# A decoder layer on one core: the second attention's output rows as three products of hi and lo halves

## The reference, cut to what matters

```python
q = (x1 @ wq.T).reshape(b, n, HEADS, HEAD_DIM).transpose(0, 2, 1, 3)
k = (x2 @ wk.T).reshape(b, m, HEADS, HEAD_DIM).transpose(0, 2, 1, 3)
v = (x2 @ wv.T).reshape(b, m, HEADS, HEAD_DIM).transpose(0, 2, 1, 3)
dots = jnp.einsum('bhnd,bhmd->bhnm', q, k) * SCALE
attn = jax.nn.softmax(dots, axis=-1)
out = jnp.einsum('bhnm,bhmd->bhnd', attn, v)
out = out.transpose(0, 2, 1, 3).reshape(b, n, DIM)
return out @ wo.T + bo
...
x = _layernorm(x + _L0_xattn_ref(x, ctx_1024, ...))
logits = xf @ router_w + router_b     # the router reads the same x
```

## Time and profile before

| | |
|---|---|
| median of 3 runs | 1996.84 us (1996.15 to 2000.22) |
| profiled execution | 1995.04 us, of which the span is 1993.4 us |
| granted TensorE clock, mean over the span | 0.978 |
| busy: PE, DVE, ACT, POOL | 1895.2, 1222.5, 884.5, 816.2 us |
| DMA | 243.53 MB |

### The profile page before, as it was taken

The page is one execution under the profiler, slowest core; times in us unless marked ns, Lnnn a source line. Parts: engine busy times, 40 slices in busy tenths (PEclk is TensorE's granted clock), DMA queues, the critical chain, the costliest instruction groups (busy, mean ns, idle before and its releaser), DMA issues.

```text
span 1993.4 us, 26331 instructions
## 1 busy us (share of the span) xinstructions
PE 1895.2 (95%) x9904; PEld 1260.5 (63%) x9904; DVE 1222.5 (61%) x2279; ACT 884.5 (44%) x1587; POOL 816.2 (41%) x735
## 2 busy tenths in 40 slices
PE   6999999989999999999999999999969999999992
PEld 4876666677655555555445545544439999888991
DVE  5566444237678788888678778778554434444433
ACT  3212322322366566666556456556714433333431
POOL 3002200100188788888667657565021222332112
PEclk8999999999999999999999999999969999999996
DMA  7102433574477477656434424422243445454316
GB/s 249 43 1 90 149 126 123 189 215 141 142 149 177 103 168 160 146 127 156 106 90 122 107 60 128 106 65 64 75 154 103 130 132 138 101 139 110 98 20 189
DMA packets 123647, 243.53 MB, mean 122 GB/s; under 512 B 11105, under 2 KB 29297, under 8 KB 119473
## 3 DMA queue, kind: packets, MB, share of 16 engines
q1 hardware_dynamic: 108560, 185.46, 31.5%
q0 software_dynamic: 13872, 54.30, 13.7%
q10 hardware_dynamic: 1088, 2.10, 0.3%
HBM read 147.15 MB, written 62.42 MB: 105 GB/s over the span
## 4 chain that ended last, share of the span: by engine, by line
PE 82%; DVE 12%; DMA 2%; issue 1%; ACT 1%; SPq 1%; POOL 1%; ACTq 0%; POOLq 0%; DVEq 0%
PE banks L1111 35%; PE banks L1370 11%; PE banks L1277 11%; PE banks L1247 10%; PE banks L1266 8%; DVE max L1544 8%; PE banks L1298 4%; PE banks L1117 2%; DMA k_parts<-out_lo 1%; DMA wv_raw<-in_wv_t 1%; DVE stats_y L1752 0%; DMA k_half<-in_xwk_t 0%; PE banks L1185 0%; DVE src_lo L1414 0%; DVE den_c L1563 0%
## 5 line engine op out<-in xcount | busy, mean ns | idle before, releaser
L1544 DVE TENSOR_REDUCE max<-banks 128x1 f32<-128x512 f32 x1024 | 627.7, 682 | 141.2 <-PE banks L1247 140.3
L2015 POOL TENSOR_TENSOR probs<-probs,probs 128x512 f32<-128x512 f32 x464 | 582.8, 1290 | 247.9 <-PE banks L1277 247.9
L1895 ACT ACTIVATE probs<-banks 128x512 f32<-128x512 f32 x1024 | 520.2, 608 | 259.5 <-PE banks L1266 258.9
L1247 PE MATMUL banks<-k_stack,q_stack 98*128 98x512 f32 x1024 | 428.1, 425 | 2.3 <-DVE max L1544 2.2
L1266 PE MATMUL banks<-q_stack,k_stack 98*128 98x512 f32 x1024 | 376.9, 398 | 2.6 <-ACT probs L1895 2.6
L1247 PEld LDWEIGHTS banks<-k_stack,q_stack 98*128 98x128 f32 x1024 | 191.6, 187 | 192.0 <-DVE max L1544 105.9
L1277 PE MATMUL banks<-probs,v_grp 128*32 128x512 f32 x2048 | 250.8, 602 | 0.0
L1266 PEld LDWEIGHTS banks<-q_stack,k_stack 98*128 98x128 f32 x1024 | 191.7, 188 | 62.4 <-ACT probs L1895 17.9
L2061 POOL DMA_INDIRECT y_rows<-eo,tok x40 | 78.1, 1952 | 218.1 <-DVE eo L1745 161.7
L1732 DVE TENSOR_TENSOR hid_lo<-hid,hid_hi 128x640 fp32r<-128x640 f32 x64 | 52.9, 826 | 142.5 <-ACT hid_hi L1960 142.5
L2025 POOL TENSOR_TENSOR x_nat<-x_nat,bxo_row 128x512 f32<-128x512 f32 x16 | 21.1, 1352 | 268.8 <-PE banks L1117 268.8
(11 more groups left out here) (228 smaller groups left out, 2702.6 us busy)
## 6 DMA issues: line engine op xcount, KB each, us to landing
k_stack<-k_parts SPq DMA_DIRECT2D x144, 256.0 KB, 5.3
w_raw<-in_L_ffn_w SPq DMA_DIRECT2D x16, 2048.0 KB, 8.3
probs<-probs POOLq DMA_DIRECT2D x31, 1024.0 KB, 10.0
q_stack<-q_parts SPq DMA_DIRECT2D x48, 256.0 KB
v_grp<-v_rows SPq DMA_DIRECT2D x48, 256.0 KB, 3.3
raw<-in_ctx_t SPq DMA_DIRECT2D x8, 1024.0 KB, 6.7
k_parts<-out_hi SPq DMA_DIRECT2D x32, 256.0 KB, 2.5
k_parts<-out_lo SPq DMA_DIRECT2D x32, 256.0 KB, 2.9
```

Of the source, the lines that this page charges most:

```text
L1247: nc.tensor.matmul(out, queries_of(t)[:, j, tile_of(k)], keys_of(t)[0:STK + SHIFT, j, mc * HALF:(mc + 1) * HALF], start=True, stop=True) \
L1544: V.reduce_max(max4[:, tiles_of(t), :, :][:, k, j, mc:mc + 1], bank(bank_of["max", t, mc, k, j]), AX.X) \
L1895: S.activation(probs_of(t, s)[:, j, :], bank(bank_of["score", t, s, j]), ACT.Exp, scale=SCALE) \
L2015: G.tensor_tensor(a[:, j, :], a[:, j, :], b[:, j, :], ALU.add).then_inc(pair_added.sem, 1)
```

## The change: what it does

- **Stage one** loads `xwo` (W_o of the second attention) into the tile that held the raw keys' weights, splits it by ACT and DVE in the third chunk of batch one's context, and stores both halves, 1 MB each, in DRAM (`store_xwo`, on SP, behind the values of (0, 3, 1)). The gate waits for these stores too. `load_xwo` at (3, 5) loads the lo half in place of the whole; `load_xwo_hi` at (8, 0) loads the hi half into the place of `probs7`.
- **Heads** are split: ACT copies 128x512 of `heads_t` into `heads_hi` (place of `probs6`, room for one half of a batch), POOL subtracts and writes `heads_lo` over `heads_t` (`split_heads`, 15 times). The last group of the last half is split per 128 tokens, by ACT and DVE (`split_tile`, 4 times).
- **rows** is three float32r matmuls a group instead of one float32 matmul. **parts** is eight float32 matmuls in column groups instead of four, on the hi and the lo halves.
- **probs:** in batch two and the last eight tiles of batch one the exponentials use six tiles in turn. By fours ends four tiles earlier.
- **Denominators** are taken in the order of their due time.
- The split of the first half's groups 0 to 2 is a generator of its own, `first_heads`, started at (7, 7), ahead of `rows_of(0, 0)` in the queue. Other splits are AT_END steps in `rows_of` or follow a `divide`.

```diff
+PLAIN_TILES = (3, 0, 8, 5, 4, 1)
+BY_FOURS = B * NG * MT - 2 * FOUR
...
-            return t * MT + s < B * NG * MT - FOUR
+            return t * MT + s < BY_FOURS
...
+                    if (b, mc, u) == (0, 0, 0):
+                        do("load_weight", "xwo")
+                    if (b, mc) == (0, 2):
+                        do("split_weight", "xwo", u)
+                    if (b, mc, u) == (0, 3, 1):
+                        do("store_xwo")
...
+        def first_heads():
+            for g in range(NG - 1):
+                yield AT_END
+                split_heads(0, 0, g)
...
             do("route_weights", b, h)
+            yield AT_END
+            next_heads(b, h, 0)
             yield WITHOUT_PE
             do("route_slots", b, h)
+            yield AT_END
+            next_heads(b, h, 1)
             for k in range(TOPK):
                 yield WITHOUT_PE
                 do("hot", b, h, k)
+                yield AT_END
+                next_heads(b, h, 2 + k)
             yield WITH_PE
             do("table", b, h, ring=next_s_bank)
...
             do("divide", t, k)
+            if t == LAST:
+                do("split_tile", b, h, k)
             if k == HT - 1:
+                if (b, h) == (1, 1) and g < NG - 1 or g == NG - 1 and not h:
+                    split_heads(b, h, g)
...
         def denominators(until):
+            pending.sort(key=lambda due: due[0])
             while pending and pending[0][0] <= until:
...
+                if (turn, s) == (7, 14):
+                    start_side(first_heads())
+                if (turn, s) == (8, 0):
+                    do("load_xwo_hi")
...
+            step = t * MT + s
+            if not by_fours(t, s):
+                return probs[PLAIN_TILES[(step - BY_FOURS) % len(PLAIN_TILES)]]
...
-                    pe.wait_ge(*divided[turn_of[b * NG + g, h], k])
+                    pe.wait_ge(*(tile_below[b, h, k] if part == LATE else heads_below[b, h, g]))
                 pe.wait_ge(*xwo_in[()])
-                accumulate(out, [(heads_t[:, g, tile_of(h * HT + k)], xwo[:, g, :]) for g in gs], start=part != LATE) \
+                pe.wait_ge(*xwo_hi_in[()])
+                cols = tile_of(h * HT + k)
+                accumulate(out, [(heads, w[:, g, :]) for g in gs
+                                 for heads, w in ((heads_hi[:, g, tile_of(k)], xwo_hi), (heads_hi[:, g, tile_of(k)], xwo),
+                                                  (heads_lo[:, g, cols], xwo_hi))], start=part != LATE) \
...
+                by_column_groups(out, [(head_w[:, g, :], heads_hi[:, g, :].bitcast(F32)) for g in range(NG)], start=False,
+                                 stop=False)
+                by_column_groups(out, [(head_w[:, g, :], heads_lo[:, g, half].bitcast(F32)) for g in range(NG)],
+                                 start=False) \
+                    .then_inc(parts_summed.sem, 1)
...
+            def split_heads(b, h, g):
+                act.wait_ge(*divided[turn_of[b * NG + g, h], HT - 1])
+                if b or h:
+                    act.wait_ge(*parts_summed[(b, h - 1) if h else (b - 1, NH - 1)])
+                else:
+                    act.wait_ge(*den_summed[B * NG - 1, 3])
+                S.activation(heads_hi[:, g, :], heads_t[:, g, h * HALF:(h + 1) * HALF], ACT.Copy) \
+                    .then_inc(heads_above.sem, 1)
...
                 if k == 0 and b:
-                    pool.wait_ge(*xo_summed[b - 1, h, HT - 1, WHOLE])
+                    pool.wait_ge(*parts_summed[b - 1, h])
...
+            def split_heads(b, h, g):
+                half = slice(h * HALF, (h + 1) * HALF)
+                pool.wait_ge(*heads_above[b, h, g])
+                G.tensor_tensor(heads_lo[:, g, half], heads_t[:, g, half], heads_hi[:, g, :].bitcast(F32),
+                                ALU.subtract).then_inc(heads_below.sem, 1)
...
+            def store_xwo():
+                sp.wait_ge(*weight_lo["xwo", NC - 1])
+                for part, tile in enumerate(w_parts["xwo"]):
+                    Q.dma_start(xwo_parts[part], tile[:, :, :].bitcast(F32)).then_inc(xwo_out.sem, 16)
+
+            def load_xwo_hi():
+                sp.wait_ge(*den_summed[B * NG - 1, 7])
+                Q.dma_start(xwo_hi[:, :, :].bitcast(F32), xwo_parts[0]).then_inc(xwo_hi_in.sem, 16)
```

More of the change, by code:

```diff
@@ L183, in program @@
         v_grp = put("v_grp", [P, MT, P])
+        probs_at = [put.at + i * 4 * HG * HALF for i in range(9)]
         probs = [put(f"probs{i}", [P, HG, HALF]) for i in range(9)]
+        heads_hi = Shelf(nc, probs_at[6])("heads_hi", [P, NG, HALF], F32R)
+        xwo_hi = Shelf(nc, probs_at[7])("xwo_hi", [P, NC, D], F32R)
         shift_rows = put("shift_rows", [SHIFT * HG * HT, P], F32R)
@@ L192, in program @@
         heads_t = put("heads_t", [P, NG, T])
-        xwo = put("xwo_t", [P, NC, D])
+        heads_lo = Shelf(nc, tail_base)("heads_lo", [P, NG, T], F32R)
+        xwo = put("xwo_lo", [P, NC, D], F32R)
         y_nat = put("y_nat", [P, HT, D])
@@ L225, in program @@
         wo, wxq = put("wo", [P, NC, D]), put("wxq", [P, NC, D])
+        k_half_at = put.at
         k_half = put("k_half", [P, HT, D])
@@ L250, in program @@
         w_parts["ck"], w_parts["cv"] = w_parts["k"], w_parts["v"]
+        w_raw["xwo"] = k_half
+        w_parts["xwo"] = [Shelf(nc, v_half_at)("xwo_first_hi", [P, NC, D], F32R),
+                          Shelf(nc, k_half_at)("xwo_first_lo", [P, NC, D], F32R)]
         put = Shelf(nc, loop_base)
@@ L308, in program @@
         bias_in = signal("bias_in", 5 * 16)
-        w_in = {n: signal(f"w{n}_in", 16) for n in ("v", "q", "o", "xq", "ck", "cv")}
+        w_in = {n: signal(f"w{n}_in", 16) for n in ("v", "q", "o", "xq", "ck", "cv", "xwo")}
         chunk_in = signals("chunk_in", 2, 16)
@@ L406, in program @@
             "load_fold": lambda: (fold_in,),
+            "store_xwo": lambda: (xwo_out,),
             "load_xwo": lambda: (xwo_in,),
+            "load_xwo_hi": lambda: (xwo_hi_in,),
+            "split_heads": lambda b, h, g: (heads_above, heads_below),
+            "split_tile": lambda b, h, k: (tile_above, tile_below),
             "zero_counts": lambda: (counts_zero,),
@@ L700, in begin_parts, with next_heads @@
             do("parts_first", b, h)
+        def split_heads(b, h, g):
+            do("split_heads", b, h, g)
+        def next_heads(b, h, g):
+            if (b, h) == (0, 0):
+                split_heads(0, 1, g)
+            elif (b, h) == (0, 1) and g < NG - 1:
+                split_heads(1, 0, g)
+        def first_heads():
+            for g in range(NG - 1):
+                yield AT_END
+                split_heads(0, 0, g)
         def rows_of(b, h):
@@ L1083, in probs_of @@
         def probs_of(t, s):
-            four, place = divmod(t * MT + s, FOUR)
+            step = t * MT + s
+            if not by_fours(t, s):
+                return probs[PLAIN_TILES[(step - BY_FOURS) % len(PLAIN_TILES)]]
+            four, place = divmod(step, FOUR)
             return probs[(four - (0, 3, 4, 7)[place]) % len(probs)]
@@ L1323, in parts @@
                 for g in range(NG):
-                    pe.wait_ge(*divided[turn_of[b * NG + g, h], HT - 1])
+                    pe.wait_ge(*(tile_below[b, h, HT - 1] if turn_of[b * NG + g, h] == LAST else heads_below[b, h, g]))
                 pe.wait_ge(*folded[()])
-                by_column_groups(bank(bank_of["parts", b, h]),
-                                 [(head_w[:, g, :], heads_t[:, g, h * HALF:(h + 1) * HALF]) for g in range(NG)],
-                                 start=False).then_inc(parts_summed.sem, 1)
+                out = bank(bank_of["parts", b, h])
+                half = slice(h * HALF, (h + 1) * HALF)
[4 more added lines that the diff above has]
+                    .then_inc(parts_summed.sem, 1)
             def logits(b, h):
@@ L1804, in split_weight @@
                     act.wait_ge(*weight_free(name))
+                if name == "xwo":
+                    act.wait_ge(*weight_lo["cv", NC - 1])
                 S.activation(w_parts[name][0][:, c, :], w_raw[name][:, c, :], ACT.Copy).then_inc(weight_hi.sem, 1)
@@ L1896, in score, with split_tile @@
                     .then_inc(exp_done.sem, 1)
+            def split_heads(b, h, g):
[6 more added lines that the diff above has]
+                    .then_inc(heads_above.sem, 1)
+            def split_tile(b, h, k):
+                act.wait_ge(*divided[LAST, k])
+                S.activation(heads_hi[:, NG - 1, tile_of(k)], heads_t[:, NG - 1, tile_of(h * HT + k)], ACT.Copy) \
+                    .then_inc(tile_above.sem, 1)
             def copy_num(t):
```

36 lines of the change are left out of this document (26 added, 10 removed).

## The result

The changed kernel takes **2016.73 us** (median of 4 runs, 2016.55 to 2017.28), beside 1996.96 us for the kernel before (4 runs, 1996.15 to 2000.22). The ratio is 1.0096, with a 95% interval of 1.008 to 1.0112: slower by 0.8 to 1.1%, some 19 us. I had forecast 1985.1 us and given "slower" a chance of 0.04. The profiled execution has a span of 2014.4 us, 21.0 over that of before.

What follows compares the result with a forecast made beforehand. PE was taken to set the time, with 82% of the last-ending chain, DVE next. Terms of rows, parts, moves, splits, stores and tail summed to -11.7 us, from 1996.84 to 1985.1 us; range 1979.5 to 1992.

Steps and rivals of the forecast that it cites:

- Slack is left, so 0 for single splits: Loop clocks with one split: pair sums are 2.3 us early for PE's pass, so POOL's subtraction costs 0.
- I estimate the sums start 1.3 to 1.5 us later: POOL in split clocks: pair sums start that much later, behind a subtraction waiting for ACT's copy.
- The double split at (8, 0), +0.7: Two splits in one clock: the sums of (8, 1) end 2.5 us later and PE waits some 0.7 us.
- POOL becomes the bound where heads are split: Rival, 15 clocks with a subtraction: sums end behind the pass and PE waits, 19.4 us, total 2003.8; chance 0.05.
- DVE takes up the saving: Rival, rows clocks: DVE leaves no gap to spare, each clock gives back 0.4 us, total 1990; chance 0.10.
- Rows, -9.6: Twelve whole tiles of rows on PE: each saves 0.80 us by three float32r products, -9.6 us.
- Early rows: Four early tiles of the last half: each goes from 2.77 to 2.11 us on PE, -2.6 us in all.
- Parts, +2.6: Three times in the loop: eight float32 matmuls in column groups take twice the 0.88 us of four, +2.6 us.
- Moves and denominators, -2.7 and 0: Loop: later side work gains 2.0 near (14, 2) and 0.7 in the last clock; denominators' extra pass and ordering cancel.
- Stores, +0.5: Stage one: 2 MB of stores of xwo ahead of the gate cost 0.5 us; rival of 1992.8, chance 0.08.
- the upper bound: Stage one: +8.2 us if key and query stores on SP's queue wait behind the 2 MB.
- Late rows: The tail: splits are hidden, and four late tiles take 2.8 us for 3.6, -0.6 us.

Runs made afterwards that it cites:

- experiment 1: Changed kernel with POOL's 128x512 subtraction of each split cut to one column, same place and waits: 2005.01 us, ratio 1.0044.
- experiment 5: Changed kernel with POOL's subtraction of a split moved behind the clock's pair sums, ACT's copy staying in place: 2003.3 us, ratio 1.0041.
- experiment 6: Changed kernel with POOL's subtraction behind the pair sums and also cut to one column: 1985.23 us, ratio 0.9948.
- experiment 7: Kernel before plus a probe behind its last output, DVE instructions beside POOL's additions: six small ones took 7.3 us, six reductions 3.65 us.
- experiment 8: Changed kernel with splits placed by hand where POOL has room, a second high-half buffer, subtraction behind the pair sums: 1983.51 us, ratio 0.9943.
- experiments 3 and 4: Kernel before with only batch two's side work moved: 1992.81 us; kernel before with only the six tiles and the denominators' order: 1995.67 us.
- experiment 11: Kernel before with only stage one's load, split and 2 MB of stores added, gate waiting for them: 1994.31 us, ratio 1.0005.
- either probe: Experiment 7, and a second probe on the kernel before where DVE comes at 16 points of POOL's instructions: small pairs took 1.52 to 2.44 us.
- experiment 12: The changed kernel run once more, nothing altered, beside the kernel before: 2015.14 us, ratio 1.01.

## Why the prediction was wrong, step by step

**The step that failed** is in the splits: "Slack is left, so 0 for single splits." I measured POOL's slack against the one reader of its sums, PE's denominator pass 2.3 us later, and for single splits it holds roughly (PE's waits for POOL are 5.2 us in all, 2.1 of them behind the double split). But POOL's gap had a second user. In before POOL stands idle ahead of the sums of nearly every clock, and DVE's small steps run there at full speed (the chain of `rsqrt_a` takes 0.16 to 0.17 us a link from 1337.29 on, and the sums start at 1339.11). The prediction's own figure for a clock's POOL work, 6.78 of 6.82 us, says that the gap goes; I took it for work that just fits. Experiments 1, 5, 6 and 7 show what comes of it: DVE's small steps take an addition each, the maxima stand behind them, PE behind the maxima, and the granted clock drops after PE's waits. In the place of 0 for the single splits and 0.7 for the double one stand +29 us, hold and work together.

**"I estimate the sums start 1.3 to 1.5 us later"** holds roughly for four splits and failed for most of the others. In before the sums start 1.25 us behind the numerators. In after they start 2.1 to 2.6 us behind those of (8, 2), (10, 2), (12, 4) and (12, 6), but 4.4 to 6.6 us behind those of (8, 0), (8, 1), (10, 0), (10, 1), (10, 3), (12, 7) and (13, 7). At the last of these POOL waited 6.27 us for ACT's copy, and there I had named the wait for the parts and gone on. Where the sums of one clock slip into those of the next, the run becomes 9.9 us long.

**The double split at (8, 0), +0.7:** PE's wait came in (8, 2), 10.54 us against 6.81 in experiment 8, so 3.7: 2.1 of it waiting, the rest at the lower clock behind it. And I overlooked a second double: two subtractions stand in a row at 1282.69 too, and behind them are the additions that make (13, 1) the longest clock.

**The rival "POOL becomes the bound where heads are split"** had place and engine right, but its time of 2003.8 counted PE waiting for POOL alone. Most of the price came by DVE. Its chance of 0.05 rested on the slack of one reader. "DVE takes up the saving" added up DVE's busy time, and that was not the matter either: DVE had no more work but was kept waiting.

**Rows, -9.6:** 12 x 0.65 = -7.8. My 2.81 us was for matmuls in a row, with 0.02 allowed for the switch back; the two edges of the block cost 0.18. Early rows: 2.28 us for 2.77, so -0.49 each and -2.0 for -2.6. **Parts, +2.6:** 1.74 us where 1.76 was forecast. **Moves and denominators, -2.7 and 0:** -3 and -1, experiments 3 and 4, the second within the noise. **Stores, +0.5:** +1, experiment 11; the upper bound was the one that the rule of the Trainium skill spoke for ("DMA: Bandwidth & Descriptors", Queues, rings and completion order), and no wait of this case shows it. **Late rows:** they start behind the identity products without a gap and take 1481.65 - 1478.37 = 3.28 us, and in before 3.53 from start to start (my 3.6 was the length of the record), so -0.2 of the -0.6.

Put together from the single runs: -3 -1 +1 -7.8 -2.0 +2.6 = -10.2, and experiment 6, where the rest of the change is alone, measures -10. The forecast, -12.4 without the 0.7 of the splits, was right for the rest within some 2 us. Experiment 8, with the same work at other places, measures -11.

**Still open** is why one DVE instruction in (13, 1) and one in (14, 1) of after are passed over at six ends of POOL's additions and let in at the seventh, where the run is over, and none in any section of either probe. In (14, 1) it changes little: experiment 1 has 14.01 us for 15.79, in pieces of 1.2 us. For (13, 1) that isn't shown: experiment 1 has 11.45 us there for 17.15. Not tried was a run with POOL's additions split up by waits in the loop itself.

## What to carry to other kernels

Before work is put on an idle engine, ask who else lives on its idle time. Slack has to be read for each user: the reader of the result, the engine that shares its memory port, and the work queued behind it. An instruction that waits for another engine must not stand ahead of periodic work; behind it and in a clock with room, the same work was free; behind it alone it was not (experiment 5). When a small edit costs much, take its work and its wait away one at a time: the two cost about the same here, and with either one gone the change was still slower than before.

## What the hardware showed unexpectedly

- A DVE instruction of 0.17 us on operands in SBUF takes 1.22 us beside back-to-back additions of GpSimd, one end of an addition for each (experiment 7); a reduction takes its 0.61 us regardless, from SBUF in experiment 7 and from PSUM in the loop.
- Two DVE instructions that take 0.17 and 0.68 us by themselves took 8.1 and 8.8 us in one piece beside such a run, at the same places in two executions (after and experiment 12).
- A switch from scores in float32r to rows in float32r costs 0.18 us in the two edges of the block of twelve matmuls.
